# A fused attention, linear-attention and expert layer: V times turned weights in high and low halves, with x kept for a batch, a shared state update and a reordered tail

## The reference, cut to what matters

```python
q, k, v = x @ Wq, x @ Wk, x @ Wv              # x: (4, 512, 256); 16 heads of q, 4 of k and v, D = 128
qs, ks = softmax(q, -1), softmax(k, -1)       # over the features
gl = log_sigmoid(k) / 16                      # the gate is made of k itself
q_r, k_r = rotary(q), rotary(k)
for t in range(n):                            # linear attention with a decaying state
    S = S * exp(gl[t])[..., None] + ks[t][..., None] * v[t][..., None, :]
    o_gla[t] = einsum('bhk,bhkv->bhv', qs[t], S)
y = softmax(causal(q_r @ k_r.T * D**-0.5)) @ v
x1 = layernorm(x + (0.5 * y + 0.5 * o_gla) @ Wo)
# eight experts of width 176, the top two of each token, weighted by the softmax of the gate
out = layernorm(x1 + sum_e comb[:, e] * ((silu(x1 @ Wg[e]) * (x1 @ Wu[e])) @ Wd[e]))
```

## Time and profile before

| | |
|---|---|
| runs | 1003.96, 1004.04, 1000.5 us; median 1003.96 |
| the profiled execution's own time | 997.87 us |
| its span, first to last instruction | 996.1 us |
| mean granted TensorE clock | 0.976 |
| TensorE, VectorE, ScalarE, GpSimd busy | 93, 67, 64, 68% |

### The profile page before, as it was taken

One profiled execution on the slowest core, in us unless ns is written; L12 is line 12 of the kernel. 1 busy time (PEld: TensorE's weight loads), 2 busy tenths in 40 slices (PEclk: granted clock), 3 DMA queues, 4 the chain that ended last, 5 costly groups with the idle time before them and its releaser, 6 DMA issues.

```text
span 996.1 us, 18579 instructions
## 1 busy us (share of the span) xinstructions
PE 925.8 (93%) x5332; PEld 720.1 (72%) x5332; DVE 663.1 (67%) x1531; ACT 636.3 (64%) x2059; POOL 677.1 (68%) x708
## 2 busy tenths in 40 slices
PE   4899999999999999999999999999999988999970
PEld 3668787878787878787878777777777765777750
DVE  4676767676767676767676969676888673331263
ACT  4667776767676767676667666766767663455451
POOL 6769796868686868687878868786768882220373
PEclk8899999999999999999999999999999998999995
DMA  7101100000000000133000000020202022234453
GB/s 251 44 27 43 38 12 12 12 12 11 11 11 11 11 11 11 63 114 99 12 12 12 12 12 12 7 77 7 72 12 72 33 78 69 85 120 125 144 173 107
DMA packets 48697, 51.08 MB, mean 51 GB/s; under 512 B 4336, under 2 KB 42608, under 8 KB 48496
## 3 DMA queue, kind: packets, MB, share of 16 engines
q1 hardware_dynamic: 45552, 41.79, 13.4%
q0 software_dynamic: 3072, 8.39, 2.7%
HBM read 31.82 MB, written 18.35 MB: 50 GB/s over the span
## 4 chain that ended last, share of the span: by engine, by line
PE 70%; DVE 9%; issue 7%; ACT 6%; POOL 4%; DMA 2%; DVEq 0%; ACTq 0%; POOLq 0%; SPq 0%
PE OA L554 11%; PE PR L455 10%; PE MS L527 9%; PE S L507 8%; PE S L536 7%; PE S L653 4%; PE OA L516 4%; PE OA L670 3%; ACT eqk L771 3%; DVE nm L947 3%; PE OA L547 3%; PE PR L479 3%; PE PR L483 2%; POOL pr L1502 2%; PE MS L468 1%
## 5 line engine op out<-in xcount | busy, mean ns | idle before, releaser
L744 ACT ACTIVATE S<-S,nm 128x128 f32<-128x128 f32 (+3 forms) x256 | 127.5, 498 | 94.5 <-DVE nm L947 91.8
L1422 POOL TENSOR_TENSOR qd<-eqk,eg 128x512 f32<-128x512 f32 x63 | 75.0, 1190 | 142.2 <-issue 129.3
L554 PE MATMUL OA<-wT,V 128*128 128x512 f32 x320 | 148.4, 594 | 0.0
L771 ACT ACTIVATE eqk<-qkv,nmx 128x128 f32<-128x128 f32 x320 | 124.3, 395 | 4.9 <-DVE nmx L1023 4.3
L947 DVE TENSOR_REDUCE nm<-S 128x2 f32<-128x256 f32 (+3 forms) x128 | 101.8, 817 | 23.5 <-PE S L507 21.8
L554 PEld LDWEIGHTS OA<-wT,V 128*128 128x128 f32 x320 | 59.6, 190 | 69.8 <-issue 69.1
L982 DVE TENSOR_TENSOR pr<-S,rl 128x256 f32<-128x256 f32 (+3 forms) x128 | 105.5, 824 | 5.1
L1399 POOL TENSOR_TENSOR rp<-qkv,cos 128x640 f32<-128x640 f32 x64 | 99.7, 1559 | 8.9 <-issue 6.5
L1402 POOL TENSOR_TENSOR rp<-rp,rt 128x640 f32<-128x640 f32 x64 | 99.5, 1555 | 5.0
L1399 POOL TENSOR_TENSOR rt<-qkv,sin 128x640 f32<-128x640 f32 x64 | 99.0, 1546 | 0.0
L1410 POOL TENSOR_TENSOR eqk<-eqk,rse 128x640 f32<-128x640 f32 x63 | 79.7, 1265 | 26.2 <-DVE rse L1066 17.9
(11 more groups left out here) (163 smaller groups left out, 2490.6 us busy)
## 6 DMA issues: line engine op xcount, KB each, us to landing
xraw<-in_x_cols SPq DMA_DIRECT2D x64, 128.0 KB, 2.2
qkv<-slot_x SPq DMA_DIRECT2D x46, 128.0 KB, 2.2
slot_y<-eqk SPq DMA_DIRECT2D x46, 128.0 KB, 1.7
gu_w<-in_wgu SPq DMA_DIRECT2D x8, 352.0 KB, 3.6
slot_x<-zero SPq DMA_DIRECT2D x2, 1280.0 KB, 5.5
stage<-in_wqkv SPq DMA_DIRECT2D x6, 384.0 KB, 3.6
acc<-in_x_rows SPq DMA_DIRECT2D x1, 2048.0 KB, 11.8
dn_w<-in_wdn SPq DMA_DIRECT2D x8, 256.0 KB, 4.3
```

The lines of the kernel that those rows point to most:

```text
L554: last = pe.matmul(OA[:, :], V[:, j, :], wT[:, j, :], start=(c == 0 and j == 0), stop=(j == c))
L744: nc.scalar.activation(S[:, h, 0:n], S[:, h, 0:n], ACT.Exp, bias=nm[:, h:h + 1], scale=1.0, accum_out=ls[:, h:h + 1]).then_inc(s_exp, 1)
L771: last = nc.scalar.activation(eqk[:, par, h * 128:(h + 1) * 128], qkv[:, c % C, h * 128:(h + 1) * 128], ACT.Exp, bias=nmx[:, h:h + 1], sca ...
```

## The change

`gather` multiplies the tiles off the diagonal in halves from group 4 on (`in_halves`: all groups but 0 to 3). ScalarE writes wT_hi, VectorE's new `weights_low` wT_lo ahead of `add_gla`, GpSimd's new `split_v` V_hi and V_lo for c < 3. x is loaded and split once for a batch entry (`renews`: in groups 3, 7 and 11), and all weight jobs are loaded ahead of that. `update_state` on VectorE keeps one operation, and ScalarE's `carry_state` makes U and Us ahead of `exps`. nabs, eabs and lnp become one tile. Groups 4 to 6 are the loop; the router keeps its steps (`route_step`). `SEND_AT` has two tiles in each of six steps. In the tail `rs2(2, 1)` goes behind `fetch(13)`, and `norm2` of the second batch entry behind the last expert tile. Buffers are moved so that all fits.

```diff
-PEEL = NG - 8
+PEEL = 7
+ROUTE = NG - 8
-HEAD = 3
+HEAD = KV
...
-        SEND_AT = {25: (0, 1), 26: (1, 3), 27: (3, 4), 28: (4, 6), 29: (6, 8), 30: (8, 12)}
+        SEND_AT = {25: (0, 2), 26: (2, 4), 27: (4, 6), 28: (6, 8), 29: (8, 10), 30: (10, 12)}
...
+        def x_tile(g, c):
+            return ((g + c // C) // KV if isinstance(g, int) else HEAD // KV) * C + c % C
+        def renews(g):
+            return isinstance(g, int) and g < NG - 1 and (g + 1) % KV == 0
+        def in_halves(g):
+            return not (isinstance(g, int) and g < HEAD)
...
@@ SyncE
-            for c in range(C):
-                load_x(0, c + 4)
-                if c:
-                    load_job(c + 1)
-            sp.dma_start(gate_w[:, :], gate).then_inc(s_gate, 16)
...
+            for j in range(2, n_attn):
+                load_job(j)
+            sp.dma_start(gate_w[:, :], gate).then_inc(s_gate, 16)
+            for c in range(C):
+                load_x(KV - 1, c + 4)
...
@@ TensorE, gather
-                for j in range(c + 1):
-                    if j < c:
-                        pe.wait_ge(s_wta, 6 * g + tri(c - 1) + j + 1)
-                    else:
-                        pe.wait_ge(s_wtd, u + 1)
-                    last = pe.matmul(OA[:, :], V[:, j, :], wT[:, j, :], start=(c == 0 and j == 0), stop=(j == c))
+                if c and in_halves(g):
+                    pe.wait_ge(s_vlo, 3 * g + c - 3 * HEAD)
+                for j in range(c):
+                    pe.wait_ge(s_wta, 6 * g + tri(c - 1) + j + 1)
+                    if in_halves(g):
+                        pe.matmul(OA[:, :], V_hi[:, j, :], wT_hi[:, j, :], start=False, stop=False)
+                        pe.matmul(OA[:, :], V_lo[:, j, :], wT_hi[:, j, :], start=False, stop=False)
+                        pe.wait_ge(s_wtl, 6 * g + tri(c - 1) + j + 1 - 6 * HEAD)
+                        pe.matmul(OA[:, :], V_hi[:, j, :], wT_lo[:, j, :], start=False, stop=False)
+                    else:
+                        pe.matmul(OA[:, :], V[:, j, :], wT[:, j, :], start=False, stop=False)
+                pe.wait_ge(s_wtd, u + 1)
+                last = pe.matmul(OA[:, :], V[:, c, :], wT[:, c, :], start=(c == 0), stop=True)
...
@@ ScalarE
+            def carry_state(g, c):
+                u = C * g + c
+                act.wait_ge(s_kvr, 3 * g + c)
+                act.wait_ge(s_eg, 2 * (u + 1))
+                later(act, s_o, u)
+                nc.scalar.activation(U[:, :], Ut[:, :], ACT.Copy, scale=eg[:, c % 2, 128:129]).then_inc(s_U, 1)
+                if c < C - 1:
+                    act.wait_ge(s_U, 3 * g + c)
+                    nc.scalar.activation(Us[:, :], U[:, :], ACT.Copy, scale=eg[:, c % 2, 129:130]).then_inc(s_us, 1)
...
+                if c:
+                    carry_state(g, c)
...
-                if q in (42, 43, 46, 47):
-                    n = (q - 42) // 4
+                if q in (42, 43):
                     for i in ((0, 1) if q % 4 == 2 else (2, 3)):
-                        norm2(n, i)
-            for n in (2, 3):
+                        norm2(0, i)
+            for n in (1, 2, 3):
...
@@ VectorE, update_state
                 if c == 1:
-                    nc.vector.tensor_copy(Ut[:, :], MS[:, 384:512]).then_inc(s_kvr, 1)
+                    nc.vector.tensor_scalar(Ut[:, :], MS[:, 384:512], into, None, ALU.mult).then_inc(s_kvr, 1)
                 else:
-                    nc.vector.tensor_tensor(Ut[:, :], MS[:, 384:512], U[:, :], ALU.add).then_inc(s_kvr, 1)
-                dve.wait_ge(s_kvr, 3 * g + c)
-                later(dve, s_o, u)
-                nc.vector.tensor_scalar(U[:, :], Ut[:, :], eg[:, 1 - c % 2, 129:130], eg[:, c % 2, 128:129],
-                                        ALU.mult, ALU.mult).then_inc(s_U, 1)
+                    dve.wait_ge(s_us, 2 * g + c - 1)
+                    nc.vector.scalar_tensor_tensor(out=Ut[:, :], in0=MS[:, 384:512], scalar=into, in1=Us[:, :],
+                                                   op0=ALU.mult, op1=ALU.add).then_inc(s_kvr, 1)
...
+            def weights_low(g, c):
+                u = C * g + c
+                later(dve, s_o, u)
+                for j in range(c):
+                    dve.wait_ge(s_wta, 6 * g + tri(c - 1) + j + 1)
+                    nc.vector.tensor_tensor(wT_lo[:, j, :], S[:, j, :], wT_hi[:, j, :].bitcast(F32), ALU.subtract).then_inc(s_wtl, 1)
...
+                if in_halves(g):
+                    weights_low(g, c)
                 add_gla(g, c)
...
@@ GpSimd
+            def split_v(g, c):
+                n = 3 * g + c + 1 - 3 * HEAD
+                nc.gpsimd.tensor_scalar(V_hi[:, c, :], qkv[:, c, 640:768], 1.0, 0.0, ALU.mult, ALU.add).then_inc(s_vhi, 1)
+                pool.wait_ge(s_vhi, n)
+                nc.gpsimd.tensor_tensor(V_lo[:, c, :], qkv[:, c, 640:768], V_hi[:, c, :].bitcast(F32), ALU.subtract).then_inc(s_vlo, 1)
...
-                if not last:
-                    x_wait(g, c + 4)
+                if in_halves(g) and c < C - 1:
+                    split_v(g, c)
                 if not (last and c >= 2):
                     rotate(g, c + 2)
-                if not last:
+                if renews(g):
+                    x_wait(g, c + 4)
                     x_split(g, c + 4)
...
-            rs2(2, 1)
             for t in range(3 * TPB, TILES):
                 fetch(t)
+                if t == 3 * TPB + 1:
+                    rs2(2, 1)
```

More of the change, by code:

```diff
@@ L100, in layer_kernel @@
         wo_lo = sb("wo_lo", [P128, H * HID], F32R)
-        stage = sb("stage", [P128, 2, WJOB], F32)
+        with nc.sbuf_tensor("stage", [P128, 2, WJOB], F32) as stage:
+            pass
+        wT_lo = sb("wT_lo", [P128, C - 1, GQ * P128], F32R)
         acc = sb("acc", [P128, TILES, HID], F32)
@@ L138, in layer_kernel @@
         pr = sb("pr", [P128, GQ, N], F32)
-        wT = sb("wT", [P128, C, GQ * P128], F32)
+        with nc.sbuf_tensor("wT", [P128, C, GQ * P128], F32) as wT:
+            pass
+        wT_hi = sb("wT_hi", [P128, C, GQ * P128], F32R)
         am = sb("am", [P128, GQ * P128], F32)
@@ L143, in layer_kernel @@
         V = sb("V", [P128, C, D], F32)
+        V_hi = sb("V_hi", [P128, C - 1, D], F32R)
+        V_lo = sb("V_lo", [P128, C - 1, D], F32R)
         U = sb("U", [P128, D], F32)
         Ut = sb("Ut", [P128, D], F32)
+        Us = sb("Us", [P128, D], F32)
         eg = sb("eg", [P128, 2, 2 * P128 + 2], F32)
@@ L149, in layer_kernel @@
         nabs = sb("nabs", [P128, D], F32)
-        eabs = sb("eabs", [P128, D], F32)
-        lnp = sb("lnp", [P128, D], F32)
+        eabs = nabs
+        lnp = nabs
         nmx = sb("nmx", [P128, GQ + 1], F32)
@@ L254, in layer_kernel @@
         s_yg = [sem(f"s_yg{i}") for i in range(4)]
+        s_us = sem("s_us")
+        s_vhi, s_vlo, s_wtl = (sem(n) for n in ("s_vhi", "s_vlo", "s_wtl"))
         s_c0, s_cb, s_nmr, s_xo, s_out = (sem(n) for n in ("s_c0", "s_cb", "s_nmr", "s_xo", "s_out"))
@@ L341, in load_x @@
             def load_x(g, c):
[L343 to L347, removed]
+                t = x_tile(g, c)
+                later(sp, s_xls, t - 1)
+                sp.dma_start(xraw[:, c % 2, :, :], x_cols.rearrange("(k p) t -> p k t", p=P128)[:, :, t * P128:(t + 1) * P128]) \
+                    .then_inc(s_xr[c % 2], 16)
             def load_job(j):
@@ L694, in _ @@
                 for c in range(C):
-                    step(g, c, last=g == NG - 1, k=C * (g - PEEL) + c)
+                    step(g, c, last=g == NG - 1, k=route_step(g, c))
             gate_up(0)
@@ L778, in gate_logs @@
                 act.wait_ge(s_cp, u + 1)
+                later(act, s_gl, u)
                 nc.scalar.activation(nabs[:, :], qkv[:, c % C, 512:640], ACT.Abs).then_inc(s_na, 1)
@@ L1329, in _ @@
                 step(0, c, first=True)
-            with dve.Fori(1, PEEL) as g:
+            for g in range(1, HEAD):
+                for c in range(C):
+                    step(g, c)
+            with dve.Fori(HEAD, PEEL) as g:
                 for c in range(C):
@@ L1431, in move_v @@
                 nc.gpsimd.tensor_copy(V[:, c, :], qkv[:, c, 640:768]).then_inc(s_v, 1)
+            def split_v(g, c):
[3 more added lines that the diff above has]
+                nc.gpsimd.tensor_tensor(V_lo[:, c, :], qkv[:, c, 640:768], V_hi[:, c, :].bitcast(F32), ALU.subtract).then_inc(s_vlo, 1)
             def x_wait(g, c):
-                u = C * g + c
-                pool.wait_ge(s_xr[c % 2], 16 * (2 * g + c // 2 + 1))
-                later(pool, s_proj, u - 3)
+                b = x_tile(g, c) // C
+                pool.wait_ge(s_xr[c % 2], 16 * (2 * b + c % C // 2 + 1))
+                later(pool, s_proj, C * (KV * b - 1) + c % C + 1)
             def x_split(g, c):
```

26 lines of the change are left out of this document (11 added, 15 removed).

## The result

The changed kernel takes 987.97 us (median of four runs, 986.32 to 992.01) against 1002.23 for the kernel before on the same chip: a ratio of 0.9864, with a 95% interval of 0.9825 to 0.9903. In a second series it was 0.9863 (0.9844 to 0.9881). So it is faster, by 1.4%, half of the 2.7% forecast. That is inside the range of 965 to 990, but outside the 966 to 984 that the forecast's own terms gave: only the part of the range that was added for the first rival holds it. The profiled execution took 992.01 with a span of 990.2, 4 us over the median where the one of before lay 4 us under its own. In this profile and in those taken on chips 0 and 7 the expert part (from the first product of expert tile 3, counted from 0, to the copy of the last tile's result) of the changed kernel and its variants took 123.6 to 130.2 us, on chip 1 115.4 to 117.3.

The account below looks back on a forecast made before the run. TensorE, busy 93% of the span, was taken as the bound; 9.9 + 8.5 + 1.5 - 2.2 + 4.5 + 4.3 = 26.5 us off 997.87, scaled to the median, gave 976, range 965 to 990.

Parts of the forecast that it names:

- the first rival: VectorE becomes the bound of the routing groups, which save nothing, and the two ends give half: 988 us, chance 0.17.
- The halves: In gather, three fp32r products at 0.23 us replace two fp32 passes: 0.165 us a tile, 9.9 us over 60 tiles.
- the rival of the subtractions blocked by GpSimd: VectorE's weights_low, slowed while GpSimd rotates, takes 1.3 us each, 5 us a group: 1040 us, slower than before, chance 0.03.
- The state update: Moving U and Us to ScalarE brings maximum, exponentials and clamp earlier, cutting TensorE's waits for gc: 8.5 us, bounds 0 and 10.
- Last group and first expert tiles: From k=25, two tiles sent per step end the sends earlier and avoid the low clock: 4.5 us, bounds -3 and 6.
- The clock's 2.7: In 832.70 to 838.40, granted clock 0.52 after TensorE's long idle time loses nearly half the stretch: 2.7 us to regain.
- the sign "granted clock 1.00 where 0.52 stood": Sign of being right: after the slot wait in the first expert tiles, TensorE's clock stays at its full level.
- the lower bound of -3: Bound of the last-group term: the longer wait in step 29 drops the clock instead, costing 3 us.
- The end: Tail: four of the last eight fetches go ahead of GpSimd's 5.41 us wait for ve: 4.3 us, bounds 2 and 5.
- x kept for a batch: 48 of 64 x loads and splits go; only group 0 gains, where TensorE waits 2.06 us for qd: 1.5 us.
- The routing groups: From group 8 VectorE also routes, and its late entries follow the added subtractions: -2.2 us, bounds 0 and -6.
- the signs of being wrong: A gap before the third product, a wait for KT_lo or rq_lo, pr late at c=1, or longer step-29 wait, lower clock.

Follow-up runs that it names:

- v_behind: The changed kernel with only split_v moved behind the rotation in GpSimd's order: 973.63 us, ratio 0.98 to the kernel before.
- before_again: The kernel before the change, unaltered, profiled once more on chip 1: 116.99 us in the expert part, 28.92 behind it.
- again: The changed kernel itself run and profiled once more on chip 1: 981.09 us, ratio 0.9863 to the kernel before.
- no_halves: The changed kernel with fp32 products everywhere, split_v and weights_low left out, the other four parts kept: 980.06 us, ratio 0.9867.

## Why the forecast was right in sign and half in size

**The halves** were right by the tile: 0.23 a product, `weights_low` 0.675 to 0.693, no wait for `wT_lo`, c=3 0.5 us shorter in each group. **The step that failed** is one sentence on what they add: "`split_v` adds two 128x128 operations on GpSimd, about 0.7 us". I priced it as time of an engine with slack, and it moved the rotation into `gl`: 0.57 us of `gl` without it, 1.38 to 1.41 with it, and c=2 of groups 4 to 6 0.8 us longer. With the rival of the subtractions blocked by GpSimd I asked the right question of the wrong operation: I went through the operations that were added and not through the ones already there whose neighbour would move. The row was at hand: U and `rk` varied threefold. The page of the Trainium skill that I cited there, "SBUF — State Buffer", section "Who interferes with whom", also says that a VectorE instruction with two inputs in SBUF contends with a GpSimd instruction that reads SBUF. It calls the ports that the two share an exclusive lock and says, beside the two-port modes, that whoever issues first keeps them for the whole instruction while the other is blocked. `gl` reads `qkv` and `nabs`; its ends 0.15 us behind the rotation's agree. What the place of `split_v` cost: 3.0 us in groups 4 to 7, 3.0 in groups 8 to 14 and 1.5 in the stretch behind, the difference of the changed kernel and `v_behind` in the table.

**The state update** was right in groups 2 and 3 (0.9 each, 48.88), but 8.5 us was too much for the whole: the experiment gives some 5.7. It was wrong in group 1: "I cost that at nothing because `pr` of that step waits for VectorE's clamp anyway". There ScalarE has a weight job too, and all three stand ahead of the exponentials; TensorE waits for `pr`:

```profile
93.48 0.39 ACT L777 ACTIVATE U<-Ut,eg 128x128 f32<-128x128 f32 x1
...
93.90 0.40 ACT L780 ACTIVATE Us<-U,eg 128x128 f32<-128x128 f32 x1
...
94.21 0.82 ACT L759 CAST wo_hi<-stage 128x768 fp32r<-128x768 f32 x1
...
97.83 1.09 PE L553 MATMUL S<-cm,pr 128*128 128x128 f32 x8 [0.42 <-DVE pr L1017]
```

Step c=1 of group 1 takes 12.10 us, 11.46 before: 0.6 us, where I had named up to 0.5 as the price without cover. The update back on VectorE doesn't mend it: the step takes 12.12 us there, since VectorE's U is the one of 1.54 us.

**Last group and first expert tiles** were the second failure and the larger one, 4.5 forecast and -1.8 measured. The clock's 2.7 was a figure of one execution, and the sign "granted clock 1.00 where 0.52 stood" didn't come: the changed kernel has 3.4 us at 0.50 in this stretch in one profile and 6.8 in the other. The sends moved as forecast, by less: the last one comes 38.9 us after the group's start for 40.1, so 1.3 earlier for the 1.8 put there, and three `split_v` in that chain measure 2.07 us (fp32 in group 15) for the 2.1 put beside them. But the wait in step 29 took it back, with the lower clock behind it, as the lower bound of -3 had it. From `before_again` to `again` the first two steps of group 15 are 3.7 us longer, 1.9 by the wait for `qd` and up to 1.7 by the clock, and what follows to expert tile 3 is 1.9 shorter. The rows of the first profile, to be set beside the earlier trace rows:

```profile
799.35 0.66 PE L500 MATMUL PR<-cm,qd 128*128 128x128 f32 x4 [3.41 <-POOL qd L1474]
...
817.57 0.96 POOL L1548 DMA_INDIRECT slot_x<-acc,sloti  x1 [0.31 <-issue]
...
822.73 0.41 PE L665 MATMUL PR<-cm,qkv 128*128 128x128 f32 x2 [0.22 <-DMA qkv<-slot_x]
...
824.59 1.62 PE L553 MATMUL S<-cm,pr 128*128 128x128 f32 x8 [1.45 <-DVE pr L1017]
```

The wait for the slots is down to 0.22 us, as forecast, but `pr` of the last step is late in its place, 1.45 us, and the wait for `qd` has grown from 1.54 to 3.41.

**The end** was right in size, 4.5 us for 4.3, and in part by luck: the experiment gives only 2.2 to 2.6 to the new order, which was the whole of the reasoning. With the old order on `v_behind` GpSimd waits 3.50 us for `ve` of tile 11, where the kernel before has 5.19 (`before_again`); what shortened it was not settled. **x kept for a batch**: step c=1 of group 0 takes 12.63 us for 13.91, so 1.3 of the 1.5, and the wait for `qd` (2.06) is gone, with one of 0.95 for `pr` in its place; no run separates that from the other parts. The rest of the 1.95 us is in step c=0, which takes 10.8 to 12.3 us in the changed kernel and its variants and 11.7 to 11.8 in the kernel before. **The routing groups** cost about the 2.2 put there, once `gl` is out of the way: groups 8 to 14 gain 6.5 for 6.4, and the halves give 3.9 in them (`v_behind` against `no_halves`) for 5.9 - 2.2 = 3.7.

The rival that gives 988, the number that came, had VectorE bind the routing groups, and the two ends give half. The second half of it came, and more: the ends gave 2.7 us of 8.8. The first didn't: the routing groups saved 3.5 us, not nothing, and 3.3 of the missing 13.3 us are in groups 4 to 7, which have no routing work and in which VectorE is idle 41 us. That the number fits to 0.03 us is luck. Two of the signs of being wrong that the prediction named did come: `pr` late at c=1 (group 1), and a longer wait in step 29 with a lower clock behind it.

## To carry to other kernels

When work is put on GpSimd ahead of something else, look at what VectorE does at the time to which that something moves: an operation with two SBUF inputs there can stand until GpSimd's is over, as `gl` did (1.41 us for 0.32), and slack on GpSimd doesn't show it. Put added work behind the long operations rather than ahead of them, and check in the durations by line, before forecasting, which operations vary threefold at the same shape. A gain built on the clock or a late transfer in one profile needs a second profile first.

## What the runs showed of the hardware that I had not expected

The same wait of TensorE, 3.41 us for `qd` in step 29, was followed by the lower clock in one profile of the changed kernel and not in the other; step c=1 of group 15 took 16.57 and 14.92 us. Of the seven profiles in which this wait is 3.33 to 3.41 us, five have the lower clock within 1 us of its end and two don't. The row and the stretch of the one that has it (`again`):

```profile
797.77 0.66 PE L500 MATMUL PR<-cm,qd 128*128 128x128 f32 x4 [3.41 <-POOL qd L1474]
```

```profile
798.49:801.90 3.41, 3.41 (x8) 1.99 (x7) 1.49 (x6) 3.30 (x14) 3.33 (x4) 0.50 0.00 0
```

The granted clock is 0.50 in that stretch, the lower of the two levels (1.2 of 2.4 GHz), right behind the wait. And the expert part of nearly the same program takes 115.4 to 117.3 us on chip 1 and 123.6 to 130.2 on chips 0 and 7 and in the profile of the result, with two to five idle times of TensorE of 1.0 to 3.5 us in it; what sets them was not settled. The kernel before had 117.67 us in the series of the result.
